# Subtracting a rounding constant on GpSimd instead of ScalarE in a fused gated attention and feed-forward kernel

## What is computed

```python
def w8a8_linear(x, w, b):              # per-row scale, integers of -127 to 127
    s  = max(max(|x|, axis=-1) / 127, 1e-8);  qx = round(x / s)
    sw = max(max(|w|, axis=1) / 127, 1e-8);   qw = round(w / sw)
    return (qx @ qw.T) * (s * sw) + b

q = w8a8_linear(layernorm(x), wq, bq); k = ctx @ wk.T + bk; v = ctx @ wv.T + bv   # 16 heads of 32
o = softmax(q @ k.T / sqrt(32) + mask) @ v
x2 = x + tanh(g_xattn) * w8a8_linear(o, wo, bo)
g, u = fp8_linear(layernorm(x2), w_gate), fp8_linear(layernorm(x2), w_up)         # 512 -> 1408
out = x2 + tanh(g_ffn) * fp8_linear(silu(g) * u, w_down)                          # 1408 -> 512
```

## Time and profile before

| What | Value |
|---|---|
| median of three runs | 590.88 us (589.11 to 592.31) |
| the profiled execution, its own time | 596.13 us |
| span of its instructions | 594.3 us |
| TensorE matmuls, busy | 490.8 us, 83% |
| VectorE, busy | 493.3 us, 83% |
| ScalarE, busy | 461.6 us, 78% |
| GpSimd, busy | 232.7 us, 39% |
| chain that ended last, by engine | DVE 36%, PE 22%, issue 12%, DMA 11%, ACT 9%, POOL 8% |
| granted TensorE clock, mean over the span | 0.93 of full |

### The profile page before, as it was taken

How to read it: one execution, slowest core, us unless ns; L and a number is a source line. 1 busy time by engine, 2 the same in 40 slices (tenths; PEclk the granted TensorE clock), 3 DMA queues, 4 the chain that set the end, 5 groups by cost and what they waited for, 6 DMA issues and landing times.

```text
span 594.3 us, 9970 instructions
## 1 busy us (share of the span) xinstructions
PE 490.8 (83%) x2994; PEld 296.2 (50%) x3030; DVE 493.3 (83%) x1254; ACT 461.6 (78%) x1129; POOL 232.7 (39%) x212
## 2 busy tenths in 40 slices
PE   1749787979998999899989998999899987862833
PEld 0645465556654655565556555654565454431311
DVE  5898896977898889987988898889687977589884
ACT  5696897979997899889988898899688977673250
POOL 4331533002472445435443544273426442441512
PEclk9965997979999999999999999999899987896979
DMA  8941524110104211320142015101520130000001
GB/s 260 389 127 38 143 71 105 38 35 19 38 19 120 62 28 25 113 73 19 24 137 50 19 24 156 36 13 30 133 48 19 25 78 10 10 10 9 16 16 72
DMA packets 61062, 39.53 MB, mean 67 GB/s; under 512 B 47569, under 2 KB 53713, under 8 KB 61009
## 3 DMA queue, kind: packets, MB, share of 16 engines
q1 hardware_dynamic: 56256, 27.47, 17.9%
q0 software_dynamic: 3328, 11.41, 6.0%
q10 hardware_dynamic: 1424, 0.01, 0.1%
HBM read 23.87 MB, written 4.19 MB: 47 GB/s over the span
## 4 chain that ended last, share of the span: by engine, by line
DVE 36%; PE 22%; issue 12%; DMA 11%; ACT 9%; POOL 8%; SPq 1%; another core or an unknown queue 1%; DVEq 0%; POOLq 0%; ACTq 0%
DVE prob L1306 5%; PE bank_s L826 4%; PE bank_t L886 4%; POOL up L462 4%; DMA unit_h<-q 3%; DMA raw_o<-in_L_xattn_wo_dram 3%; DMA q_last<-raw_o 3%; POOL up L452 3%; DVE q L1207 3%; DVE ts L1483 3%; ACT prob L653 3%; PE bank_g L1061 2%; DVE t_sb L1202 2%; DVE t_sb L1246 2%; PE bank_u L846 2%
## 5 line engine op out<-in xcount | busy, mean ns | idle before, releaser
L653 ACT ACTIVATE prob<-prob,neg_max 128x256 f32<-128x256 f32 x256 | 126.7, 499 | 10.9 <-DVE neg_max L1306 10.9
L1306 DVE CUSTOM_DVE_ANT_0 prob<-bank_s,mask_sb 128x256 f32<-128x256 f32 x256 | 95.6, 420 | 37.9 <-PE bank_t L886 25.4
L662 ACT ACTIVATE probT<-bank_t 128x512 f32<-128x512 f32 x128 | 73.4, 592 | 28.6 <-PE bank_t L886 26.0
L826 PE MATMUL bank_s<-kf,qf 32*128 32x256 f32 x512 | 77.0, 420 | 14.7 <-DVE neg_max L1306 13.9
L886 PE MATMUL bank_t<-ident,prob 128*128 128x128 f32 x512 | 82.0, 290 | 7.9 <-ACT prob L653 6.4
L452 POOL TENSOR_TENSOR up<-up,wgu_scale 128x512 f32<-128x512 f32 (+1 forms) x42 | 52.1, 1241 | 89.4 <-ACT up L633 89.4
L886 PEld LDWEIGHTS bank_t<-ident,prob 128*128 128x128 f32 x512 | 60.0, 146 | 40.2 <-issue 18.2
L826 PEld LDWEIGHTS bank_s<-kf,qf 32*128 32x128 f32 x512 | 46.0, 193 | 41.4 <-DVE neg_max L1306 22.5
L462 POOL TENSOR_TENSOR up<-gate,up 128x512 f32<-128x512 f32 (+1 forms) x42 | 60.0, 1429 | 4.3 <-DVE gate L1361 2.3
L467 POOL TENSOR_TENSOR x<-x,y 128x512 f32<-128x512 f32 x14 | 19.9, 1425 | 84.8 <-DVE y L1496 84.8
L653 ACT ACTIVATION_READ_ACCUMULATOR prob<-prob,neg_max 128x1 f32 x256 | 49.0, 192 | 0.0
(11 more groups left out here) (232 smaller groups left out, 1071.9 us busy)
## 6 DMA issues: line engine op xcount, KB each, us to landing
x_in<-in_x_dram SPq DMA_DIRECT2D x8, 512.0 KB, 3.4
c_in<-in_ctx_dram SPq DMA_DIRECT2D x8, 512.0 KB
out_dram<-x POOLq DMA_DIRECT2D x7, 512.0 KB, 3.6
mask_sb<-in_mask_BxSxS_ff_dram SPq DMA_DIRECT2D x8, 256.0 KB, 2.9
t_sb<-in_L_ffn_w_down_dram SPq DMA_DIRECT2D x2, 704.0 KB, 5.5
t_sb<-in_L_ffn_w_down_dram POOLq DMA_DIRECT2D x2, 704.0 KB, 7.7
kf<-in_L_xattn_wq_dram SPq DMA_DIRECT2D x1, 1024.0 KB, 10.8
wkT<-in_L_xattn_wk_dram SPq DMA_DIRECT2D x1, 1024.0 KB, 13.4
```

What stands on the lines that cost most here:

```text
L653: ins = act.activation(prob[:, head_par, t, :], prob[:, head_par, t, :], ACT.Exp, bias=neg_max[:, head_par, t:t + 1], scale=-1.0, accum_ou ...
L662: act.activation(probT[:, (slot + 3) % 4, :, :].rearrange("p a b -> p (a b)"), T_BANK[(slot + 1) % 2][:, :], ACT.Copy).then_inc(s["turned_ ...
L826: ins = pe.matmul(S_BANK[(slot + i) % 2][:, t * L:(t + 1) * L], qf[r:r + 32, hb, c, t * P:(t + 1) * P], kf[r:r + 32, hb, c, :], start=(t = ...
L1306: ins = dve.tensor_tensor_reduce(prob[:, hp, t, :], S_BANK[hp][:, t * L:(t + 1) * L], mask_sb[:, hb, t, :], -1.0, 3.4e38, ALU.add, ALU.min ...
```

## The change

ScalarE's instructions of `x_int` and `o_int` (two 128x512 tiles each) become GpSimd's, as `tensor_scalar` with a subtraction; ScalarE keeps everything else in its order. In GpSimd's program `x_int(2)` comes behind `x_var(0)` in steps 0 and 1 and behind `x2_var(2)` in the steady steps, and `o_int(0)` is the first work of a steady step and of the tail.

```diff
@@ pool @@
+                def x_int(slot):
+                    for t in range(NT):
+                        pool.wait_ge(s["x_rounded"], 2 * b + t + 1)
+                        pool.tensor_scalar(x_ints(b)[:, t, :], centred(b)[:, t, :], ROUND, None, ALU.subtract).then_inc(s["x_ints"], 1)
+
+                def o_int(slot):
+                    for t in range(NT):
+                        pool.wait_ge(s["o_rounded"], 2 * (b - 2) + t + 1)
+                        pool.tensor_scalar(ints_o[:, t, :], rows[:, t, :], ROUND, None, ALU.subtract).then_inc(s["o_ints"], 1)
...
             def first_step_order(k):
-                k.load(4); k.load(6); k.x_var(0); k.load(8); k.load(10); k.x_plus_bias(4); k.load(14); k.load(12)
+                k.load(4); k.load(6); k.x_var(0); k.x_int(2); k.load(8); k.load(10); k.x_plus_bias(4); k.load(14); k.load(12)
             def second_step_order(k):
-                k.load(2); k.load(0); k.x_plus_bias(4); k.x_var(0); k.load(6); k.load(4); k.load(8)
+                k.load(2); k.load(0); k.x_plus_bias(4); k.x_var(0); k.x_int(2); k.load(6); k.load(4); k.load(8)
             def steady_step_order(k):
-                k.x_var(0); k.x2_add(1); k.x2_var(2); k.up_scale(6); k.gate_up(6); k.up_scale(7); k.gate_up(7)
+                k.o_int(0); k.x_var(0); k.x2_add(1); k.x2_var(2); k.x_int(2); k.up_scale(6); k.gate_up(6); k.up_scale(7); k.gate_up(7)
             def tail_order(k, e):
-                k.x2_add(1); k.x2_var(2); k.up_scale(6); k.gate_up(6); k.up_scale(7); k.gate_up(7); k.up_scale(8)
+                k.o_int(0); k.x2_add(1); k.x2_var(2); k.up_scale(6); k.gate_up(6); k.up_scale(7); k.gate_up(7); k.up_scale(8)
@@ act @@
-                def x_int(slot):
-                    for t in range(NT):
-                        act.wait_ge(s["x_rounded"], 2 * b + t + 1)
-                        act.activation(x_ints(b)[:, t, :], centred(b)[:, t, :], ACT.Identity, bias=-ROUND).then_inc(s["x_ints"], 1)
-
-                def o_int(slot):
-                    for t in range(NT):
-                        act.wait_ge(s["o_rounded"], 2 * (b - 2) + t + 1)
-                        act.activation(ints_o[:, t, :], rows[:, t, :], ACT.Identity, bias=-ROUND).then_inc(s["o_ints"], 1)
...
             def steady_step_order(k):
-                k.head_probT(0); k.o_int(0); k.head_exp(0); k.head_exp(1); k.head_exp(2); k.x_centre(0); k.group_oT(1)
-                k.head_probT(1); k.head_exp(3); k.head_probT(2); k.x_round(2); k.x_int(2); k.k_out_0(3); k.head_probT(3)
+                k.head_probT(0); k.head_exp(0); k.head_exp(1); k.head_exp(2); k.x_centre(0); k.group_oT(1)
+                k.head_probT(1); k.head_exp(3); k.head_probT(2); k.x_round(2); k.k_out_0(3); k.head_probT(3)
```

More of the change, by code:

```diff
@@ L24 @@
 SpBlocks = namedtuple('SpBlocks', """x_load ctx_load mask_load x_turn o_turn x2_turn t_turn""")
-PoolBlocks = namedtuple('PoolBlocks', """load x_var x2_add x2_var x_plus_bias up_scale gate_up out_add out_store""")
-ActBlocks = namedtuple('ActBlocks', """pro_round_q unit_mag_0 gate_tanhs pro_round_o wo_scaled oqT_high k_out_1 x_int o_int tT_high up_copy t_mag_0 t_mag_1
+PoolBlocks = namedtuple('PoolBlocks', """load x_var x_int o_int x2_add x2_var x_plus_bias up_scale gate_up out_add out_store""")
+ActBlocks = namedtuple('ActBlocks', """pro_round_q unit_mag_0 gate_tanhs pro_round_o wo_scaled oqT_high k_out_1 tT_high up_copy t_mag_0 t_mag_1
 t_mag_2 head_exp head_probT group_oT o_round k_out_0 x_centre x_round x2_mag_0 x2_mag_1 q_high gate_tanh unit_copy
@@ L473, in blocks @@
                 return PoolBlocks(
-                    load, x_var, x2_add, x2_var, x_plus_bias, up_scale, gate_up, out_add, out_store)
+                    load, x_var, x_int, o_int, x2_add, x2_var, x_plus_bias, up_scale, gate_up, out_add, out_store)
             def first_step_order(k):
-                k.load(4); k.load(6); k.x_var(0); k.load(8); k.load(10); k.x_plus_bias(4); k.load(14); k.load(12)
+                k.load(4); k.load(6); k.x_var(0); k.x_int(2); k.load(8); k.load(10); k.x_plus_bias(4); k.load(14); k.load(12)
             def second_step_order(k):
-                k.load(2); k.load(0); k.x_plus_bias(4); k.x_var(0); k.load(6); k.load(4); k.load(8)
+                k.load(2); k.load(0); k.x_plus_bias(4); k.x_var(0); k.x_int(2); k.load(6); k.load(4); k.load(8)
             def steady_step_order(k):
-                k.x_var(0); k.x2_add(1); k.x2_var(2); k.up_scale(6); k.gate_up(6); k.up_scale(7); k.gate_up(7)
+                k.o_int(0); k.x_var(0); k.x2_add(1); k.x2_var(2); k.x_int(2); k.up_scale(6); k.gate_up(6); k.up_scale(7); k.gate_up(7)
                 k.up_scale(8); k.gate_up(8); k.up_scale(9); k.gate_up(9); k.up_scale(10); k.up_scale(11); k.gate_up(10)
@@ L722, in blocks @@
                     pro_round_q, unit_mag_0, gate_tanhs, pro_round_o, wo_scaled, oqT_high, k_out_1,
-                    x_int, o_int, tT_high, up_copy, t_mag_0, t_mag_1, t_mag_2, head_exp, head_probT, group_oT,
+                    tT_high, up_copy, t_mag_0, t_mag_1, t_mag_2, head_exp, head_probT, group_oT,
                     o_round, k_out_0, x_centre, x_round, x2_mag_0, x2_mag_1, q_high, gate_tanh, unit_copy, unit_mag)
@@ L728, in first_step_order @@
                 k.unit_mag(6); k.x_centre(0); k.unit_copy(5); k.k_out_0(3); k.k_out_1(4); k.pro_round_o(3); k.x_round(2)
-                k.x_int(2); k.wo_scaled(6); k.unit_copy(7); k.unit_mag(8); k.unit_mag(10); k.q_high(7); k.q_high(8)
+                k.wo_scaled(6); k.unit_copy(7); k.unit_mag(8); k.unit_mag(10); k.q_high(7); k.q_high(8)
                 k.unit_copy(9); k.unit_copy(11); k.head_exp(12); k.head_exp(13); k.head_probT(14); k.unit_mag(12)
@@ L737, in second_step_order @@
                 k.head_probT(3); k.unit_copy(3); k.head_probT(4); k.k_out_0(3); k.head_exp(4); k.head_exp(5)
-                k.k_out_1(4); k.x_round(2); k.x_int(2); k.group_oT(5); k.head_probT(5); k.unit_mag(4); k.unit_copy(5)
+                k.k_out_1(4); k.x_round(2); k.group_oT(5); k.head_probT(5); k.unit_mag(4); k.unit_copy(5)
                 k.head_probT(6); k.head_exp(6); k.head_exp(7); k.head_probT(7); k.head_probT(8); k.head_exp(8)
@@ L758, in tail_order @@
             def tail_order(k, e):
-                k.head_probT(0); k.o_int(0); k.head_exp(0); k.head_exp(1); k.head_exp(2); k.head_probT(1); k.group_oT(1)
+                k.head_probT(0); k.head_exp(0); k.head_exp(1); k.head_exp(2); k.head_probT(1); k.group_oT(1)
                 k.head_exp(3); k.head_probT(2); k.head_probT(3); k.head_probT(4); k.head_exp(4); k.head_exp(5)
```

## The result

The changed kernel takes 623.42 us, the median of four runs (622.2 to 624.49), against 591.6 us before: a ratio of 1.054 with a 95% interval of 1.0494 to 1.0586, some 32 us. The forecast was slower by 2.3%, 604.5 us with a range of 596 to 614. The direction was right; the size was less than half of what came, and the result lies outside the range.

The account below looks back on a forecast made before the run. TensorE was taken to wait for the transposes of both moved pieces. Terms of 12.25 + 0.85 + 0.5 + 0 gave +13.6 us on the profiled 596.13, carried over to the median as 604.5 us, range 596 to 614.

Parts of the forecast that it names:

- Which waits bound: Output projection and q projection: TensorE waits for the transposes of o_int and x_int, 1.06 and 0.42 us, so later integers delay it.
- The price D: GpSimd's subtraction of a constant on one 128x512 tile: estimated 0.64 us, with ends at 0.62 and 1.29.
- rival D: GpSimd's operation near its upper end, 1.29 us: each transpose 0.65 us later, +8.5 us, 613.0 us; chance 0.14.
- The term of x: x_int behind x2_var in steady steps: first transpose and q projection 1.85 us later in each.
- The term of the output path: o_int behind the store's issue in steady steps: transpose 1.2 us later, output projection 0.6 us later, five times.
- In the first steady step: No store before o_int: 1.0 us gained at the output projection, 1.85 lost for x_int, +0.85 us in all.
- The clock, rival C: TensorE's clock falls after the longer waits in all six steps, 1.28 us each: +7.7, 612.2 us; chance 0.22.
- The sum for D = 0.64: Whole kernel, all terms added: +13.6 us; +8.5 with unknown terms at their lower ends, +21.3 at their upper ends.
- Hidden as forecast: Steps 0 and 1: transposes keep their place and later weight loads cost nothing, bounds -1 and +3 us.
- That projection itself: Tail's output projection: starts at 490.8 against 490.28, +0.5 us, bounds -0.4 and +1.2.
- Rivals A and B: Whole kernel: faster through ScalarE's relief, 584 us, chance 0.06; or no change, delay absorbed by later waits, 591 us, chance 0.08.
- ScalarE's relief: 28 activations of 0.62 us and two in step 0 leave ScalarE, about 18.6 us of work.

Follow-up runs that it names:

- the runs with short operations: Changed kernel with GpSimd's subtractions cut to 168 of 512 columns, 1.016, or replaced by copies of all columns, 1.011, both against the kernel before.
- the copy: Changed kernel with GpSimd copying all 512 columns to bf16 instead of subtracting: 1.011 to the kernel before, +6.6 us.

## Why the prediction was right in direction and wrong in size

- **Which waits bound, right in the main.** The output's transposes ended last at TensorE, and the waits grew at just the two places named. Each piece moved alone brought a loss, and moving `o_int` forward a gain. For x the reading of the earlier trace rows was wrong: the 0.42 us a step were the weight load's, and the matmuls of the q projection did not wait. The transposes of x landed just as TensorE came to them, with no slack to lose, so the conclusion held.
- **The price D, the step that failed.** "I take 0.64, since the moved operation reads one tile and not two, and the memset's slope is that of one stream." The slope of a memset is that of a copy; the operation with a constant has three times that, 2.55 ns an element. D is 1.50 us and lies outside the two ends as well: the two-input product, 1.25 to 1.29 us, is no upper bound. No row of the kernel before had the operation on a wide tile, and the two rows that were nearest by shape told nothing about its form. With 1.50 in rival D's sum, where each 0.65 us of D brought 8.5, the prediction would have been 604.5 + 11.2 = 615.7 us, an estimate; that leaves some 8 of the 623.4. The Trainium skill says in "GPSIMD Engine Reference", section 3.1, that a body of at most two operations runs at 1.03 cycles an element at 1.2 GHz, an estimate of 0.33 us for the step from 128 to 512 columns. The copy took 0.32 more, which agrees; the subtraction of a constant took 0.98 more, and the measurement decides. Section 4.1 of that page gives elementwise work on a tile to VectorE and not to GpSimd; no run here moved the subtraction to VectorE.
- **The term of x.** From the end of `x2_var` to the q projection 3.15 us passed before and 279.62 - 273.62 = 6.00 after, **2.85 us a step where the term said 1.85**. Six times, that is 17 us. The difference comes apart in this step: D is 0.86 longer; the second half, which was to add nothing (true for D = 0.64), adds 0.51, since the second transpose starts at 276.98 and not at 276.47; and from there the pair of transposes let TensorE start 0.37 sooner than before (4.34 - 0.51 = 3.83 us from the first one's issue, 4.20 before).
- **The term of the output path**, 0.6 us: TensorE's wait grew by 0.9 to 1.8 us. At that place alone (`o_int` only) the six steps lost 9.7 us, 1.6 a step. In the first steady step a gain of 1.0 us was forecast; TensorE waited 1.24 us there for the transposes, where it had not waited before.
- **The clock, rival C.** It was set beside rival D with 0.22 and priced at one fall a step, +7.7 us. It goes together with D, since D made the waits longer. The clock fell at most of the long waits in the first profile of the changed kernel and at three in the second; this can cost as much as 8 to 10 us, and differs from run to run. C and D together, each on top of the forecast's 13.6, would have been 604.5 + 7.7 + 8.5 = 620.7 us; the prediction named such a sum and left it outside its range, which ended at 614.
- **The sum for D = 0.64** was +13.6, with ends at +8.5 and +21.3; the runs with short operations gave +10 and +6.6. That is near, a little high: the q projection waits 1.0 us in them and not 2.3. In the fourth steady step of the copy the difference is 0.42 for the misread wait, 0.16 for a subtraction that starts sooner behind `x2_var` (the first transpose 0.64 us behind its end and not 0.80), 0.37 for the same quicker pair of transposes, and 0.3 for TensorE, which comes to the q projection later itself.
- **Hidden as forecast:** steps 0 and 1 (the first output projection at 135.60 us after and 136.10 in the second profile of before), and what follows the tail's output projection (102.9 us to the end of the span after, 104.0 before). That projection itself waited 1.89 us for its transposes, where +0.5 was forecast. Rivals A and B fell. ScalarE's relief was 15 us of work and not 18.6, and it brought no time.
- **Open:** that `x_int` alone costs nearly as much as both. In that run the stretch from q projection to up projection grew by 11.1 us over six steps, in the changed kernel by 6.1 in its first profile and not at all in its second. Where the clock falls differs, but why was not tried, and `x_int` alone (379.4 us for the six steps) even lies above the second profile of both (373.9).

## What to carry to other kernels

An idle engine is no free one: what counts is when its result is there, behind what stands in its queue, and 15 us taken off a busy engine gave nothing because the tile went to a DMA for which TensorE was already waiting. If no row shows the operation itself, form and width both, its price is open upwards; five instructions behind the end of a kernel settle it. And where a wait of TensorE grows, the clock may fall with it: here a longer wait and a slower clock came together in some steps and runs, so price their sum too, and profile a kernel twice before a few us are put down to the clock.

## What the runs showed that was not expected

- On GpSimd, by itself, subtracting or multiplying by a constant takes 1.50 us on 128x512, subtracting a tile 1.25, copying or casting 0.60; two constants 1.92. The output's type does not matter.
- TensorE's clock fell to 1.2 GHz after a wait of 2.45 us, and did not after another wait of 2.44 us in the same run. With matmuls that do nothing useful in the waits it stayed up in all six steps; the ratio was 1.040 against 1.054, but the six steps took no less than in the better of two profiles without them (373.0 and 373.9 us).
- The first steps of the kernel before differ by 5 us between two profiles, and the six steps behind them by less than 1 in 349. The six steps of the changed kernel differ by 8.8.
